# Layer norm spread over the K and V groups of a transformer layer: statistics, rows and columns of a subtile in three successive groups

## The reference

```python
xn = _layernorm(x, axis=-1)
x = x + _L0_attn_ref(xn, W_q, W_k, W_v, W_o) + _L0_ffn_ref(xn, w_gate, w_up, w_down, s_gate, s_up, s_down)
```

## Time and profile before

| | |
|---|---|
| median of 3 runs | 3573.27 us (3490.6 to 3616.72) |
| the profiled execution | 3487.79 us, span of its slowest core 3486.1 us |
| spans of the 8 cores in it | 3471.1 to 3486.1 us |
| TensorE busy | 3399.9 us of the span, 98% |
| mean granted TensorE clock | 0.995 to 0.996 |
| TensorE busy from 0 to 140 us | 88.1 us, clock 0.90 |
| TensorE busy from 140 to 240 us | 99.3 us, clock 1.00 |

### The profile page before, as it was taken

One profiled execution on the slowest core, in us unless ns is written; L12 is line 12 of the kernel. 1 busy time (PEld: TensorE's weight loads), 2 busy tenths in 40 slices (PEclk: granted clock), 3 DMA queues, 4 the chain that ended last, 5 costly groups with the idle time before them and its releaser, 6 DMA issues.

```text
span 3486.1 us, 49034 instructions; the slowest of 8 cores (3471.1 to 3486.1 us)
## 1 busy us (share of the span) xinstructions
PE 3399.9 (98%) x15824; PEld 1542.6 (44%) x15824; DVE 2391.4 (69%) x3226; ACT 1205.7 (35%) x1437; POOL 1624.7 (47%) x1521
## 2 busy tenths in 40 slices
PE   5899999999999999999999999999999999999999
PEld 2444444444444444444444444444444444444444
DVE  5468777767776777677743677677776777677633
ACT  4421133443334333443311133443344333433111
POOL 1134445555555555555511155555555555555311
PEclk9999999999999999999999999999999999999999
DMA  8555476698668776667697666676667666676864
GB/s 214 156 114 145 152 209 181 169 151 170 181 179 144 155 191 178 143 143 195 183 225 124 145 180 184 150 169 176 183 153 164 176 181 154 142 183 181 210 127 85
DMA packets 180568, 578.98 MB, mean 166 GB/s; under 512 B 28256, under 2 KB 54880, under 8 KB 176096
## 3 DMA queue, kind: packets, MB, share of 16 engines
q0 software_dynamic: 132768, 484.53, 60.2%
q1 hardware_dynamic: 47552, 91.32, 8.2%
HBM read 318.64 MB, written 109.05 MB: 123 GB/s over the span
## 4 chain that ended last, share of the span: by engine, by line
PE 89%; DMA 4%; DVE 3%; issue 2%; ACT 1%; POOL 1%; DVEq 0%; POOLq 0%; ACTq 0%; SPq 0%
PE ps_f L109 54%; PE ps_f L113 8%; PE ps_s L109 7%; PE ps_av L109 6%; PE ps_k L109 4%; PE ps_s L113 3%; PE ps_av L113 3%; PE ps_m L109 2%; DMA x_t<-x_nat 1%; DMA wab<-wd 1%; PE ps_m L113 1%; DMA outT<-ost 1%; DVE st L368 1%; POOL kst L473 0%; ACT expT L990 0%
## 5 line engine op out<-in xcount | busy, mean ns | idle before, releaser
L109 PE MATMUL ps_f<-xop,wab 128*128 128x512 bf16 x6272 | 1545.2, 379 | 15.4 <-DVE th L750 7.1
L990 ACT ACTIVATE expT<-ps_s,bias,isq_sb 128x1024 bf16<-128x1024 f32 x512 | 616.6, 1204 | 1092.9 <-PE ps_s L113 1043.3
L1007 POOL TENSOR_TENSOR acc<-acc,expT 128x1024 f32<-128x1024 f32 x320 | 688.5, 2152 | 634.9 <-ACT expT L990 581.4
L109 PEld LDWEIGHTS ps_f<-xop,wab 128*128 128x128 bf16 x6272 | 612.1, 98 | 761.2 <-issue 28.2
L109 PE MATMUL ps_f<-fop,wab 128*128 128x512 bf16 x3136 | 770.8, 380 | 12.9 <-DVE fop L766 4.5
L109 PEld LDWEIGHTS ps_f<-fop,wab 128*128 128x128 bf16 x3136 | 306.8, 98 | 386.4 <-issue 19.6
L113 PE MATMUL ps_f<-xop,wab 128*128 128x512 bf16 x896 | 339.6, 379 | 0.0
L814 DVE TENSOR_TENSOR ps_f<-ps_f,usum 128x512 f32<-128x512 f32 x384 | 264.8, 690 | 72.1 <-PE ps_f L113 64.9
L791 ACT ACTIVATE ost<-ps_f,sd_sb 128x512 f32<-128x512 f32 x256 | 174.5, 686 | 306.6 <-DVE ps_f L814 195.4
L822 DVE TENSOR_TENSOR usum<-usum,ps_f 128x512 f32<-128x512 f32 x384 | 260.0, 677 | 13.3 <-PE ps_f L113 13.1
L745 ACT ACTIVATE th<-ps_f,sgh 128x512 f32<-128x512 f32 x256 | 170.4, 686 | 229.5 <-DVE ps_f L814 194.9
(11 more groups left out here) (116 smaller groups left out, 3782.9 us busy)
## 6 DMA issues: line engine op xcount, KB each, us to landing
wab<-wg POOLq DMA_DIRECT2D x299, 512.0 KB, 4.9
wab<-wu POOLq DMA_DIRECT2D x296, 512.0 KB, 4.9
wab<-wd POOLq DMA_DIRECT2D x146, 512.0 KB, 4.8
outT<-ost POOLq DMA_DIRECT2D x127, 512.0 KB, 7.7
x_t<-x_nat SPq DMA_DIRECT2D x16, 1024.0 KB, 9.2
wo_sb<-wo POOLq DMA_DIRECT2D x32, 512.0 KB, 9.4
ring<-wq POOLq DMA_DIRECT2D x16, 512.0 KB, 7.8
q_scr<-kst SPq DMA_DIRECT2D x64, 128.0 KB, 2.8
```

The source lines that it names most:

```text
L109: streams["t"].append(lambda t, o=out, l=lhsT, r=rhs, a=start, z=stop: t.matmul(o, l, r, start=a, stop=z, skip_group_check=True))
L990: e = op("s", lambda s, kk=k, gg=g, rr=r, tt=t: s.activation(expT[:, kk, :], ps_s[:], AF.Exp, bias=bias[:, gg, rr, tt:tt + 1], scale=isq_s ...
L1007: summed = op(eng, lambda x, d=acc, o=one, kk=k: x.tensor_add(d[:], o, expT[:, kk, :]))
```

## The change

Four things are different. `ln_stage` is gone; in its place are `look(i)` (statistics), `rows(i)` (scale and rows of one subtile) and `cols(i)` (columns, one half copied by ACT and one by DVE), which stand in three successive groups: in one group the columns of one subtile, the rows of the next and the statistics of the one after. The table `beside` says what stands where. Second, `v_rows` appends its copy and its store ahead of the pieces of layer norm instead of behind them, and has four `vst` buffers. Third, the copies of the columns of subtiles 4 to 15 are divided between ACT and DVE. Fourth, the requests: subtiles 8 to 11 are requested after the first two groups of K of tile 1, 12 to 15 behind the rows of 8 to 11; V's weights wait for subtile 5 instead of 7; cos and sin of tiles 2 and 3 are requested after groups 8 and 13, and the first weights of Q that need subtile 15 after group 13 instead of 11.

```diff
--- before.py
+++ after.py
@@ -160,8 +160,8 @@
         rpb = [place("rpb%d" % i, [128, TS], F32, a_sm + 4 * KB * i + 2 * KB) for i in range(2)]
         sqb = [place("sqb%d" % i, [128, TS], BF16, a_sm + 8 * KB + KB * i) for i in range(2)]
         kst = [place("kst%d" % i, [128, TS], BF16, a_sm + 10 * KB + KB * i) for i in range(2)]
-        vst = [place("vst%d" % i, [128, TS], BF16, a_et + KB * i) for i in range(2)]
-        at = [a_et + 2 * KB]
+        vst = [place("vst%d" % i, [128, TS], BF16, a_et + KB * i) for i in range(4)]
+        at = [a_et + 4 * KB]
 
         def small(name, shape, dtype=F32):
             size = 4 if dtype == F32 else 2
@@ -223,7 +223,7 @@
         l_wv = mksem("l_wv")
         l_cs = lanes("cs", NT)
         l_kst = lanes("kst", 2)
-        l_vst = lanes("vst", 2)
+        l_vst = lanes("vst", 4)
         l_spill = lanes("spill", 2)
         l_xop = lanes("xop", 7)
         l_kv = lanes("kv", 2)
@@ -433,7 +433,7 @@
             rp_free = [None, None]
             sq_free = [None, None]
             st_free = [None, None]
-            vs_free = [None, None]
+            vs_free = [None] * 4
             behind = []
 
             def norms(left):
@@ -483,13 +483,13 @@
                 done = mm_last(ps_s[:, vb, :], xn[t][:, DC - 1, sub * 128:sub * 128 + 128],
                                wv_sb[:, DC - 1, :], False, True)
                 norms(1)
+                wait("s", done, vs_free[sub])
+                s_free[vb] = op("s", lambda s: s.activation(vst[sub][:], ps_s[:, vb, :], AF.Copy))
+                wait("y", s_free[vb])
+                vs_free[sub] = dma("y", l_vst[sub], lambda y: y.dma_start(
+                    vscr[:, :, tc, :], vst[sub][:].rearrange("p (g d) -> p g d", g=G)))
                 for f in between:
                     f()
-                wait("s", done, vs_free[vb])
-                s_free[vb] = op("s", lambda s: s.activation(vst[vb][:], ps_s[:, vb, :], AF.Copy))
-                wait("y", s_free[vb])
-                vs_free[vb] = dma("y", l_vst[vb], lambda y: y.dma_start(
-                    vscr[:, :, tc, :], vst[vb][:].rearrange("p (g d) -> p g d", g=G)))
                 return done
 
             def keys(t, g, between=()):
@@ -498,30 +498,26 @@
                     proj.release(g, done)
                 return done
 
-            def ln_stage(t, j):
-
-                i = 4 * t
-                if j in (0, 1, 2, 3):
-                    if j == 2:
-                        ln_apply(i + 1, pair_scale[0])
-                        load_next(i + 1)
-                    ln_stats(i + j)
-                    if j % 2:
-                        pair_scale[0] = ln_scale((i + j) // 2 % 2, 0, 2, st6_free[1])
-                        ln_apply(i + j - 1, pair_scale[0])
-                        load_next(i + j - 1)
-                if j == 4:
-                    ln_apply(i + 3, pair_scale[0])
-                    load_next(i + 3)
-                if j >= 4:
-                    ln_transpose(i + j - 4, ("s", "s"))
-
-            def load_next(i):
-                if i + 4 < 16:
-                    load_x(i + 4)
-
-            pair_scale = [None]
-            stage = lambda t, j: (lambda: ln_stage(t, j))
+            seen = {}
+
+            def look(i):
+
+                def run():
+                    seen[i] = ln_stats(i)
+                return run
+
+            def rows(i):
+
+                def run():
+                    ln_apply(i, ln_scale(i // 2 % 2, i % 2, 1, seen[i]))
+                    if 8 <= i < 12:
+                        load_x(i + 4)
+                return run
+
+            def cols(i):
+
+                return lambda: ln_transpose(i, ("s", "v"))
+
             for i in range(4):
                 stats = ln_stats(i)
                 ln_apply(i, ln_scale(i // 2 % 2, i % 2, 1, stats))
@@ -534,26 +530,35 @@
             load_cs(1)
 
 
-            ln_stage(1, 0)
-            ln_stage(1, 1)
-            keys(0, 0, [stage(1, 2), stage(1, 3)])
-            wait("g", x_loaded[7])
+            look(4)()
+            rows(4)()
+            keys(0, 0)
+
+            wait("g", x_loaded[5])
             wv_loaded = dma("g", l_wv, lambda g: g.dma_start(wv_sb[:], wvd))
-            keys(0, 1, [stage(1, 4)])
-            keys(0, 2, [stage(1, 5)])
-            ln_stage(1, 6)
-            keys(0, 3, [stage(1, 7)])
+            keys(0, 1, [cols(4), look(5)])
+            keys(0, 2, [rows(5), look(6)])
+            keys(0, 3, [cols(5), rows(6), look(7)])
+            rows(7)()
+            cols(6)()
+            cols(7)()
             for dst, src in ((sg_sb, sgd), (su_sb, sud), (sd_sb, sdd)):
                 scales = dma("y", l_const, lambda y, d=dst, s=src: y.dma_start(d[:], s))
 
             groups = [(keys, 1, k) for k in range(4)] + [(v_rows, t, k) for t in (0, 1) for k in range(4)]
             groups += [(what, t, k) for t in (2, 3) for what in (keys, v_rows) for k in range(4)]
+            beside = {4: [look(8)], 5: [rows(8), look(9)], 6: [cols(8), rows(9), look(10)],
+                      7: [cols(9), rows(10), look(11)], 8: [cols(10), rows(11), look(12)],
+                      9: [cols(11), rows(12), look(13)], 10: [rows(13), look(14)], 11: [cols(12), rows(14), look(15)],
+                      12: [cols(13), rows(15)], 13: [cols(14)], 14: [cols(15)]}
             for n, (what, t, k) in enumerate(groups):
-                v_last = what(t, k, [stage(2 + n // 8, n % 8)] if n < 16 else ())
-                if n == 4:
-                    load_cs(2)
-                    load_cs(3)
-                if n == 11:
+                v_last = what(t, k, beside.get(n, ()))
+                if n < 2:
+                    load_x(2 * n + 8)
+                    load_x(2 * n + 9)
+                if n in (8, 13):
+                    load_cs(2 + n // 13)
+                if n == 13:
                     wait("g", x_loaded[15])
                     proj.request(RING - 1)
             wait("v", scales)
```

## The result

| | before | changed |
|---|---|---|
| runs that the ratio compares | 3487.9, 3490.1, 3490.6 us | 3469.1, 3470.3, 3471.2 us |
| profiled execution, its slowest core's span | 3486.1 us | 3469.7 us |
| spans of the 8 cores, median | 3478.4 us | 3462.7 us |
| median of all six runs | 3531.9 us | 3693.95 us |

The ratio of the times is 0.9945, with a 95% interval of 0.9922 to 0.9967: 19 us faster, forecast 15.5 (0.9956); that is well within the 2% that the forecast called no change that can be told. The ratio leaves out three of each kernel's six runs, those over 1.5% above the kernel's fastest: 3573, 3617 and 4087 us before, and 3917, 4129 and 4145 of the changed kernel, in which the cores of one die or of both ran at a mean granted clock of 0.82 to 0.93.

What follows compares the result with a forecast made beforehand. TensorE bounds the kernel after K and V, so only its earlier steady part counts: 2.0 (tile 1) + 12.6 (V) + 0.9 (K of tile 2) = 15.5 off 3487.8, 3472 us; range 3460 to 3602.

Steps and rivals of the forecast that it cites:

- The bound: After K and V TensorE stays the bound, so the end comes nearer only by what TensorE gains before.
- V's groups: V of tiles 0 and 1: no wait for stores, ACT slightly late; 34.5 us instead of 47.1, 12.6 less.
- K of tile 2: K of tile 2 loses one subtile's transposes to V's stage: 0.9 us less.
- Tile 1: Layer norm of tile 1 beside K of tile 0: K of tile 1 at 70.0 against 71.69, V 2.0 us earlier.
- The turn-taking: Subtiles 5 to 7 take turns with K's work from 43.24 to 70.0, so K of tile 1 gains only 1.7.
- The clock: First group of K of tile 1 after little TensorE work: 5.92 us instead of 3.40, a loss taken as 2.5.
- V's weights against subtiles 6 and 7: Rival: V's weights, asked for at 43.3, hold up subtiles 6 and 7; gain 0 to loss of 5, 3488 to 3493; 6%.
- The requests of 8 to 11 at no cost: Subtiles 8 to 11, asked for at about 77 and 81, land 7 to 9 us before they are wanted; cost 0.
- The buffers: V's groups: a vst buffer comes back after four groups instead of two, so the 8.47 us wait for stores should go.
- handshakes decide: Rival: each full turn costs TensorE 1 to 1.5 us, or tile 1's chain ends at 74; 3480 us; 14%.
- everything hidden: Rival: clock up at K of tile 1 and transposes never wait; gain 20.5, 3467 us; 12%.
- not handed on: Rival: something behind K and V, or another core being slowest, takes the gain back; 3488 us; 8%.

Runs made afterwards that it cites:

- experiment 5: Changed kernel with both copies of columns of subtiles 4 to 15 on ScalarE again; 3476.9 us.
- experiment 3: Kernel before, with only V's copy ahead of the pieces of layer norm and four vst buffers; 3499.3 us.
- experiment 9: Changed kernel with statistics and rows of subtiles 5 to 7 in one piece beside K's second group, V's weights behind subtile 7; 3464.0 to 3467.5 us, ratio 0.9937.
- experiment 1: Changed kernel with V's weights asked for behind subtile 7 again instead of 5; 3470.9 us.
- experiment 7: Changed kernel with 24 extra matmuls, their result not read, between the transposes of subtiles 6 and 7; 3468.8 us.
- experiment 6: Changed kernel with subtiles 8 to 11 asked for behind the rows of 4 to 7 again, about 30 us earlier; 3473.6 us.
- experiment 4: Changed kernel with two vst buffers instead of four; 3470.1 us.
- experiment 8: Changed kernel with tile 1 as in the kernel before (statistics in pairs), V's weights behind subtile 7, copies of columns still divided; 3471.3 us.

## Why the prediction was right or wrong

**The range: wrong, as far as the median goes.** The median of all six runs, 3693.95, lies outside 3460 to 3602. The step that failed is the range's upper end. It was made from the spread of the three runs shown, 3616.7 less the gain, as if they bounded how long an execution can take. They did not: the next three of the kernel before had one of 4087, and three of the changed kernel's six took 3917, 4129 and 4145, so that its median fell between 3471 and 3917. The point of 3472 against 3469 to 3471 in the runs compared, and 15.5 us against 19.3 (interval 11.5 to 27 us), were right.

**The bound: right.** What TensorE gains up to Q is what the kernel gains. Q starts 14.0 us earlier as median, and from Q to the end the cores took 3279 to 3289 us before and 3281 to 3289 now, with medians of 3284.0 and 3284.2: nothing is taken back. The spans are 15.7 shorter as median, and 16.4 on the slowest core. Why the compared times differ by 19.3, 3 more than that, was not followed up.

**V's groups: right, the last tenths by luck.** The forecast had 32.05 for TensorE's own work and 2.5 for ScalarE; measured 34.5. Four subtiles' transposes start about 0.55 behind the end of the group ahead, 2.2 in all (the rows show 0.38 to 0.40 of it as a wait), and one sum in ps_m takes 0.22. The forecast had five such waits of 0.5 and left the sum out; the two slips cancel. The reason holds as well: ScalarE's turn is late next, 4.89 us against 4.34, and in experiment 5 0.92 more of it became 0.92 more wait. The base was core 7's 47.1; the median core had 48.4, which makes the gain 13.9 instead of 12.6. The prediction did not divide it; experiments 3 and 5 do: 7.0 by buffers and the copy first, 4.2 by the spreading, 2.7 by the divided copies.

**K of tile 2:** forecast 0.9 for the moved transposes; K of tile 2 to Q shrank by 0.9 (60.6 to 59.7). Right.

**Tile 1: wrong, the gain did not come.** "K of tile 1 starts at 70.0, against 71.69", with V 2.0 earlier. As median it starts 1.6 later, V 1.2 later, and with the scatter of K's start (above) a loss is not told from nothing. The step that failed is the base; the chain built on it and the clock held.

- *The base.* 43.24, at which the statistics of subtile 5 start, and 71.69 are those of core 7, on which subtile 5 landed at 43.2. On the other cores of the kernel before its statistics started at 35.6 to 39.8. On core 3, subtile 5's statistics and K of tile 1:

```profile
39.43 2.47 DVE L368 BATCH_NORM_STATS2 st<-x_t 128x6 f32<-128x512 f32 x4 [5.78 <-DMA x_t<-x_nat]
```

```profile
67.23 3.40 PE L109 MATMUL ps_k<-xn,ring 128*128 128x512 bf16 x15 [1.73 <-ACT xn L413]
```

  One core, the slowest of the eight, was taken as the kernel. On it x is late, so that what now stands ahead of the statistics of 5 costs nothing. On the others it does: these statistics stand behind VectorE's copy of the columns of 4, whose transposes stand behind K's second group. On core 5 of the changed kernel subtile 5 was asked for at 18.2 and landed at 34.5, and its statistics started at 42.6:

```profile
L337 SPq DMA_DIRECT2D x_t<-x_nat x1: 328/328/328, 18.2 to 18.2; - x1
...
DMA to landing us min/median/max: 16.3/16.3/16.3
```

```profile
41.89 0.69 DVE L411 COPY xn<-ps_t 128x1024 bf16<-128x1024 bf16 x1 [2.15 <-PE ps_t L405]
42.61 2.47 DVE L368 BATCH_NORM_STATS2 st<-x_t 128x6 f32<-128x512 f32 x4
```

  As medians they started at 39.0 before and at 41.6 now.
- *The turn-taking.* The chain that was worked out ran as forecast: 26.8 us from the statistics of 5 to K of tile 1 by hand, 25.9 to 26.3 on the seven cores where subtile 7 was in time, against 28.3 as median before, with undivided copies. What it gains there, 2.4, the later start of the statistics takes back. One piece in its place is 1.7 us faster still (experiment 9 against 1); the prediction did not set the two orders side by side.
- *The clock.* Taken at 2.5; experiment 7 measures 2.4. Right, and so was the gain from K's sums without waits: from K of tile 1 to V it took 17.5 before, 17.0 now, and 14.7 where the clock was up.

**V's weights against subtiles 6 and 7.** The rival's mechanism happened, at a small part of its price: subtile 7 came at 59.8 on core 4 where it was wanted at 54.6, against 61 and 57.4 in the working. It cost that core 5.3 us of waiting and, by experiment 1 and the traces named there, 4 us at K's start. The page *DMA: Bandwidth & Descriptors* of the Trainium skill (Queues, rings and completion order) says that each DMA engine takes turns between the queues by packets. The trace agrees in that both queues moved data from 46 to 62 us, but not in equal parts: 587 packets, 0.90 MB and 18.0% of the engines' time on SP's queue, 128 packets, 1.82 MB and 68.4% on the other. Half of the bytes for each, as the prediction worked out, would have brought 7 at 52.9.

**The requests of 8 to 11 at no cost: right** (experiment 6). **The buffers:** "the wait for stores should go" was right, but with the pieces spread it would nearly have gone with two as well (experiment 4). **The rivals "handshakes decide", "everything hidden" and "not handed on"** did not occur; the idle of 0.4 a turn lies between the first two.

## What to carry to other kernels

- Where several engines serve one that bounds the kernel, put into each of its groups one equal portion of each engine's side work and add up each engine's turn: the stage then runs at the largest turn, here 4.89 us against 4.75 by hand. But spread only what has time. Ahead of a stage that waits for the last portion, taking turns with other work makes it late: 1.7 us here, between experiments 1 and 9.
- Work out a wait for data on several cores, not on the slowest alone: there the data is late (43.2 us here, where the other cores had it at 35 to 40), and an order that wastes time on the others looks free. Take two traces of one kernel before you call a start earlier or later: K of tile 1 moved by 1.5 us, between the kernel before and experiment 3, without any change of the instructions ahead of it.
- A stretch of idle on TensorE costs its idle and then more for the clock, here 2.0 to 2.9 us on the eight cores of the changed kernel; real work that falls near the end of it keeps the clock up (K's fourth group in experiment 8, but only if it is not put on the path, as in 9).
